# Attention of a graph network: one tile in four of the weighing moved from VectorE to ScalarE

## What is computed

```
scores = sum(q_dst * kt, -1) / scale * mu                  # per edge and head
e   = exp(scores - segment_max(scores, dst)[dst])          # softmax over the edges of one node
s   = segment_sum(e, dst)
w   = e / (s[dst] + 1e-10)
agg = segment_sum(V[src] * w[..., None], dst)              # the weighing and the sums
```

## Time and profile before

| | |
|---|---|
| median of three runs | 5523.89 us |
| profiled execution | 5507.77 us |
| its span | 5506.1 us |
| TensorE busy | 4233.9 us, 77% of the span |
| VectorE busy | 3805.5 us, 69% |
| GpSimd busy | 3222.0 us, 59% |
| ScalarE busy | 1627.1 us, 30% |
| L1619 (weighing), VectorE, L2a | 240 + 108 instructions, 1201 and 1203 ns each |
| L1619, VectorE, L3a | 116 instructions, 1205 ns each |

### The profile page before, as it was taken

One profiled execution on the slowest core, in us unless ns is written; L12 is line 12 of the kernel. 1 busy time (PEld: TensorE's weight loads), 2 busy tenths in 40 slices (PEclk: granted clock), 3 DMA queues, 4 the chain that ended last, 5 costly groups with the idle time before them and its releaser, 6 DMA issues. The chain is left out here.

```text
span 5506.1 us, 69197 instructions
## 1 busy us (share of the span) xinstructions
PE 4233.9 (77%) x19341; PEld 3318.3 (60%) x19341; DVE 3805.5 (69%) x8692; ACT 1627.1 (30%) x3998; POOL 3222.0 (59%) x3108
## 2 busy tenths in 40 slices
PE   4666666377777578887987888898788888878886
PEld 4554544354444566665886666688666667756665
DVE  6644444275555569998536999853699996679998
ACT  3443433230000332222343222234322223422221
POOL 2388888717777467774126777413677750067773
PEclk9888888789999889998998999999899999989998
DMA  4488888736666478886027888512688862077774
GB/s 160 102 124 125 124 123 123 110 121 211 210 209 211 157 249 246 249 245 179 23 79 229 249 248 246 177 44 74 218 247 250 247 178 65 16 231 243 245 237 150
DMA packets 525142, 959.78 MB, mean 174 GB/s; under 512 B 87702, under 2 KB 299876, under 8 KB 523955
## 3 DMA queue, kind: packets, MB, share of 16 engines
q0 software_dynamic: 224512, 549.90, 40.0%
q1 hardware_dynamic: 300130, 404.93, 22.8%
q10 hardware_dynamic: 128, 0.52, 0.0%
HBM read 718.56 MB, written 236.50 MB: 173 GB/s over the span
## 5 line engine op out<-in xcount | busy, mean ns | idle before, releaser
L1464 POOL DMA_INDIRECT L2a_rows<-kv_rows,typed_index x960 | 909.1, 947 | 299.8 <-issue 277.3
L1771 PE MATMUL L2a_sums<-L2a_weighted,L2a_hot 128*128 128x264 f32 x2784 | 844.5, 444 | 200.7 <-DVE L2a_weighted L1619 175.1
L867 POOL DMA_INDIRECT sum_rows<-L0s_rows,L0s_row_of x464 | 724.1, 1561 | 152.7 <-issue 120.4
L1771 PEld LDWEIGHTS L2a_sums<-L2a_weighted,L2a_hot 128*128 128x128 f32 x2784 | 578.0, 216 | 358.6 <-DVE L2a_weighted L1619 212.8
L1760 PE MATMUL L2a_query<-x,L2a_turned 128*128 x2784 | 706.1, 399 | 44.3 <-ACT L2a_turned L1714 26.9
L1760 PEld LDWEIGHTS L2a_query<-x,L2a_turned 128*128 128x128 f32 x2784 | 545.6, 201 | 145.2 <-issue 49.4
L1286 POOL DMA_INDIRECT L1s_rows<-rows,index x464 | 452.7, 976 | 269.3 <-ACTq L87 128.2
L1464 POOL DMA_INDIRECT L3a_rows<-feature_rows,index x464 | 439.2, 947 | 168.8 <-issue 144.5
L1002 PE MATMUL L0s_message<-features,L0s_share 128*128 x928 | 313.8, 497 | 287.4 <-ACT L0s_share L967 287.4
L1464 POOL DMA_INDIRECT hold<-kv_rows,typed_index x432 | 409.2, 947 | 184.8 <-issue 172.7
L1722 ACT ACTIVATE L2a_hot<-L2a_hot 128x512 f32<-128x512 uint8 x348 | 218.8, 630 | 1009.3 <-PE L2a_sums L1771 1009.3
(11 more groups left out here) (430 smaller groups left out, 8337.8 us busy)
## 6 DMA issues: line engine op xcount, KB each, us to landing
code_rows<-L1s_code SPq DMA_DIRECT2D x232, 256.0 KB, 2.9
L3a_code<-code_rows SPq DMA_DIRECT2D x116, 512.0 KB, 3.9
L0s_wide<-source_rows SPq DMA_DIRECT2D x116, 256.0 KB, 4.2
L2a_turn<-turned_rows SPq DMA_DIRECT2D x87, 256.0 KB, 4.4
L2a_pens<-mask_rows SPq DMA_DIRECT2D x87, 256.0 KB
L2a_hot<-hot_rows SPq DMA_DIRECT2D x87, 256.0 KB, 3.9
kv_rows<-L2d_key_rows SPq DMA_DIRECT2D x50, 384.0 KB, 2.6
kv_rows<-L2d_value_rows SPq DMA_DIRECT2D x150, 128.0 KB, 2.5
```

The source lines that it names most:

```text
L867: pool.indirect_dma_start(c.sum_rows[u], bass.IndirectOffsetOnAxis(ap=row_of[:, 4 * n + u:4 * n + u + 1], axis=0), rows[n % ring][:, u, :] ...
L1464: pool.indirect_dma_start(rows[n % ring][:, u, :], None, table, bass.IndirectOffsetOnAxis(ap=index_of[:, t:t + 1], axis=0)).then_inc(lande ...
L1771: last = pe.matmul(sums[(m * WP + j) % held][:, :], hot[quad % 2][:, j % 2 * 2 + k, :], weighted[:, 2 * j + k, :], start=k == 0, stop=k == 1)
```

## The change

`weigh` on VectorE covers the first three tiles of a quad. A new function `weigh_fourth` on ScalarE covers the fourth, one copy for each head, scaled by that head's weight, which `soften` has left in column 32 of the head. Eight copies then raise a new semaphore, `fourth_ready`. GpSimd waits for it too before it uses a ring buffer again, and TensorE waits for it ahead of the second pair of each quad (j odd).

```diff
@@ gpsimd
                 wait(pool, weighted_ready, n - ring + 1)
+                wait(pool, fourth_ready, n - ring + 1)
@@ vector, weigh
-                    weighted[:, 4 * q:4 * q + 4, :].rearrange("p k (h d) -> p k h d", h=H)[:, :, :, 0:HD],
-                    rows[quad % ring][:, :, values:values + D].rearrange("p k (h d) -> p k h d", h=H),
+                    weighted[:, 4 * q:4 * q + 3, :].rearrange("p k (h d) -> p k h d", h=H)[:, :, :, 0:HD],
+                    rows[quad % ring][:, 0:3, values:values + D].rearrange("p k (h d) -> p k h d", h=H),
...
@@ scalar
+            def weigh_fourth(m, q):
+                if m >= 0:
+                    quad, u = m * WQ + q, 4 * q + 3
+                    wait(act, prob_ready, m + 1)
+                    for h in range(H):
+                        own = slice(h * HC, h * HC + HD)
+                        last = act.activation(weighted[:, u, own], rows[quad % ring][:, 3, values + h * HD:values + (h + 1) * HD],
+                                              ACT.Copy, scale=weighted[:, u, h * HC + HD:(h + 1) * HC])
+                    last.then_inc(fourth_ready, 1)
@@ scalar, the loop
                 soften(m)
+                weigh_fourth(m, 0)
                 widen(m, 2)
                 turn(n + 1, 2)
+                weigh_fourth(m, 1)
                 widen(m, 3)
                 turn(n + 1, 3)
+                weigh_fourth(m, 2)
+                weigh_fourth(m, 3)
                 widen(n, 0)
@@ tensor, total
                     wait(pe, weighted_ready, quad + 1)
+                    if j % 2:
+                        wait(pe, fourth_ready, quad + 1)
                     wait(pe, hot_ready, quad + 1)
```

More of the change, by code:

```diff
@@ L1452, in attend @@
                 "added", "rescaled"))
+        fourth_ready = st.sem("fourth_ready")
         block = st.block()
@@ L1619, in weigh @@
                 dve.tensor_tensor(
-                    weighted[:, 4 * q:4 * q + 4, :].rearrange("p k (h d) -> p k h d", h=H)[:, :, :, 0:HD],
-                    rows[quad % ring][:, :, values:values + D].rearrange("p k (h d) -> p k h d", h=H),
-                    prob_ps[:, 4 * q * H:4 * (q + 1) * H].rearrange("p (k h) -> p k h", h=H).unsqueeze(3).broadcast_to(
-                        [P, 4, H, HD]), ALU.mult
+                    weighted[:, 4 * q:4 * q + 3, :].rearrange("p k (h d) -> p k h d", h=H)[:, :, :, 0:HD],
+                    rows[quad % ring][:, 0:3, values:values + D].rearrange("p k (h d) -> p k h d", h=H),
+                    prob_ps[:, 4 * q * H:(4 * q + 3) * H].rearrange("p (k h) -> p k h", h=H).unsqueeze(3).broadcast_to(
+                        [P, 3, H, HD]), ALU.mult
                 ).then_inc(weighted_ready, 1)
```

## The result

The changed kernel takes 5826.76 us, the median of four runs (5817.65 to 5835.17), against 5524.85 us before. The ratio is 1.054, with a 95% interval of 1.0528 to 1.0558: slower, by 302 us. The profiled execution took 5820.88 us, its span is 5819.2 us.

A forecast was written before the change was run, and what follows sets the result against it. VectorE was taken as the present pace, with a ring of handoffs through TensorE close behind that takes over: 21.69 us plus 1.3 for the clock, 23.0 a group, adding 273 us, hence 5790 us; range 5610 to 5970.

The forecast's parts named there:

- the term for the clock: TensorE's first sums and the `ask` behind them, partly at lower clock: 1.3 us a group added.
- the ring: Handoffs through TensorE's fixed order, one `sequence` to the next: 21.69 us a group at full clock, setting the pace.
- Set 0 and set 3 hidden, sets 1 and 2 not: ScalarE's sets of eight copies, 1.80 us each: quads 0 and 3 covered by other work, 1 and 2 delay TensorE.
- TensorE's two waits: TensorE waiting for ScalarE's copies ahead of the second sum of quads 1 and 2: about 1.5 us each, every group.
- The lower level: TensorE at 1.2 instead of 2.4 GHz: two first sums take 3.57 us instead of 1.88.
- the rival of no clock loss: Lower clock falls on TensorE's waits or covered steps: 21.69 us a group, 5630 us; chance 0.16.
- The clock falling more often: One new TensorE wait costs another 1.7 us each group: 24.7 us a group, 5979 us (both waits 6176); chance 0.14.
- VectorE's saving: Four shorter weighings save VectorE 1.0 us a group; as a rival, this comes through: 5438 us, chance 0.08.
- the lower end of a set: Cheapest eight ScalarE copies, from the unscaled 8-column copy, 186 ns, starting every 0.09 us: 0.84 us.
- upper end from gaps: Dearest eight ScalarE copies, 0.249 us each, taken as the average of 50-column copies with their gaps: 2.07 us.
- The floor of the gathers: GpSimd's 16 gathers a group at 1.25 us each: a group takes at least 20.0 us.

The follow-up runs named there:

- the spilled copies: Changed kernel, but VectorE weighs all four tiles and ScalarE's copies go to an unread spare tile, TensorE not waiting for them: 5523.37 us, ratio 0.9995.
- the early order: Changed kernel with ScalarE's sets 0 and 1 right behind `soften`, set 2 behind `turn(n+1, 2)`, set 3 behind `turn(n+1, 3)`: 5450.48 us, ratio 0.9865.
- Moving one set: Changed kernel with only set 1 moved up behind set 0; sets 2 and 3 stay behind `turn(n+1, 3)`: 5631.35 us, ratio 1.0194.
- The last kernel: Changed kernel with the early order of the four sets and ScalarE's `drop` ahead of `widen(m, 1)`: 5437.22 us, ratio 0.9845.

## Why the prediction was right, step by step

It forecast 5790 us; it was 5827, 302 us more than before against 273 in the sum. The mechanism was right, step by step; the term for the clock was too small, and a part of the closeness is luck, as the sixth point below says. From the group shown above:

| term of the ring | predicted, us | measured, us |
|---|---|---|
| `sequence` to `zz` (5455.87 to 5462.01) | 6.11 | 6.14 |
| `zz` to the first sum (5462.01 to 5464.66) | 2.68 | 2.65 |
| `total(m, 0)`, `total(m, 1)` (5441.22 to 5444.47) | 1.88 | 3.25 |
| `ask`, `turn`, set 1 (to 5449.20) | 4.38 | 4.73 |
| `total(m, 3)`, `flatten` (to 5450.27) | 1.18 | 1.07 |
| `ask`, `turn`, set 2 (to 5454.69) | 4.48 | 4.42 |
| `total(m, 5)` (to 5455.87) | 0.98 | 1.18 |
| the clock, apart | 1.3 | within the third and fourth term: 1.37 + 0.32 |
| sum | 23.0 | 23.44 |

5464.66 is the start of the next group's first sum, 23.44 us after 5441.22; the mean over the stage is 23.14.

- *The busiest engine is not the bound.* Shown by the spilled copies and by the early order: the same work on ScalarE costs 302 us, nothing, or less than nothing (-74 us against before), by where it stands.
- *Set 0 and set 3 hidden, sets 1 and 2 not.* TensorE's two waits of 1.63 us were forecast at 1.5. Moving one set gave back 1.7 us a group, moving both 3.2 (376 / 116).
- *The clock.* The lower level was in the ring, as forecast: taking it away from the first sums gave back 1.06 us a group with 0.03 of the clock still lost, and the rival of no clock loss (5630) is out. In the kernel before the same loss was covered: of its groups one with the lower level (5110.86 to 5132.08) and one without (5068.31 to 5089.53) both take 21.22 us. The size was too small. 1.3 us were put in, less than the 1.5 of the average because TensorE's wait is 0.25 us shorter; in the group shown it is 1.37 + 0.32 = 1.69, and over the first 25 groups 23.33 - 21.76 = 1.57. The shorter wait did not lower it.
- *The clock falling more often* was given 0.14, for every group. It happened in two of the first 25 groups of the last stage, and there it cost what the rival said, 1.7 us (25.12 instead of 23.44). In most groups the sums behind both waits of 1.63 us ran in 1.13 us, at the full level. The mean granted clock in the last stage stayed at 0.93 and does not show the two groups.
- *VectorE's saving* was sized right (0.94 us a weighing, forecast 0.95) and lost, since it lies in a stretch that is not on the ring, but for one weighing a group (the second term).
- *The sum was 29 us short, and it could have been more.* The mean of all four stages is 23.20 us a group against 23.0, which is 23 us over 116 groups. The three L2a stages took 20.40 before, not 20.47, which is 6 us more over 87. Behind the 23.20 stand errors that partly cancel. A full group of the last stage is 21.76 us at full clock (21.69 in the forecast) plus 1.57 for the clock (1.3), 23.33 in all; the two short groups at the end of each stage, which the forecast did not have, bring the mean back by 0.2. That 23.0 came so near to 23.14 is luck to that extent. The steps without the clock are right to 0.2 us each: the last one was 1.18 instead of 0.98, the two before it together 0.17 less.
- *Two slips without effect.* By its own terms the lower end of a set is 7 x 0.09 + 0.186 = 0.82 us, not 0.84. And 37.8 / 152 = 0.249 us is busy time with no gaps in it, so it was no upper end from gaps; the sets measured 1.79 to 1.81.
- *The floor of the gathers*, 20.0 us, was used only in the rival. The last kernel runs at it, with VectorE waiting for a gather; that the gathers alone hold it there was not tested by taking some away.

## What to carry to other kernels

Before moving work to an idle engine, write down what that engine waits for just ahead of the new place and who waits for it just behind: in this kernel an engine that works through its list in order and hands over between two others lengthened their ring by all that was put between. Put such work where its inputs are ready and ahead of the next wait, not behind it; here the order of a few lines was worth 376 us, five times the 74 us by which the kernel with the well-placed copies beats the kernel before. And add up the ring for each place, with the lower clock level of TensorE included when its waits come into it.

## What the runs showed of the hardware

- Six extra transposes (0.82 us) in a wait of 1.7 us made the sums behind it run at 2.4 instead of 1.2 GHz in every group of the last stage and the kernel 123 us faster. After two other waits of 1.63 us in the same group, with sums and an `ask` between them, the level stayed at 2.4 GHz in most groups and fell in some (2 of 25 without the transposes, 7 of 25 with them): the length of one wait did not tell it. What exactly does is not settled here.
- A stretch at the lower level cost its 1.7 us in full where the matmuls were on the ring, and nothing where they were not (groups of 21.22 us with it and without it in the kernel before).
- ScalarE's small scaled copies start every 0.21 us and take 307 ns each, 8 in 1.79 to 1.81 us; one copy of 256 columns without a scale takes 0.40. Eight scaled pieces cost 4.5 times as much as one unscaled piece of the same size. Most of it is the number of pieces, not the scale: one copy of 256 columns with a scale took 0.50 us.
- ScalarE and VectorE reading the same buffers and writing to the same tile at once did not slow VectorE. In the group shown the two weighings beside a set of copies took 0.94 and 0.95 us, the two without 0.93 and 0.94.
